# CoPE attention: the table selection as two row groups of 64 rows, with two table products and one addition moved on TensorE

## The chip, the cores and the metric

One Trainium2 chip, one of its cores. The metric is the device time of one execution of the whole program in microseconds (us), lower is better. Each kernel is run several times and the median counts.

## The reference

One decoder layer in float32: self-attention, cross-attention with contextual position encoding (CoPE), and a routed feed-forward layer. The change is in the cross-attention: batch 4, 1024 queries, 1024 keys, 16 heads of width 32, 64 positions.

```python
def cope(query, attn_logits, pos_emb):
    npos_max = pos_emb.shape[-1]
    gates = jax.nn.sigmoid(attn_logits)
    pos = jnp.flip(jnp.cumsum(jnp.flip(gates, axis=-1), axis=-1), axis=-1)
    pos = jnp.minimum(pos, npos_max - 1)
    pos_ceil = jnp.ceil(pos).astype(jnp.int32)
    pos_floor = jnp.floor(pos).astype(jnp.int32)
    logits_int = jnp.einsum('bhqd,dn->bhqn', query, pos_emb)
    logits_ceil = jnp.take_along_axis(logits_int, pos_ceil, axis=-1)
    logits_floor = jnp.take_along_axis(logits_int, pos_floor, axis=-1)
    w = pos - pos_floor
    return logits_ceil * w + logits_floor * (1.0 - w)
...
logits = jnp.einsum('bhqd,bhkd->bhqk', Q, K) / jnp.sqrt(jnp.asarray(d, Q.dtype))
scores = jax.nn.softmax(logits + cope(Q, logits, pos_emb), axis=-1)
out = jnp.einsum('bhqk,bhkd->bhqd', scores, V)
```

So every (query, key) pair looks up the curve `logits_int[query, :]` at its own position `pos`, between two neighbouring entries.

## The kernel before, in words

The program runs its stages one after the other; the CoPE attention (`build_cope_attention`) is the long one. It works through 128 **quads** (64 pairs of batch and head, two halves of 512 queries each), and a quad has four **slots** t = 0 to 3 of 128 queries. One number n = 4 i + t counts the slots. A PSUM or SBUF tile has 128 key rows as partitions and eight key groups along the free side.

Eight neighbouring keys share one *anchor*, a coarse position. For each query a small table is made by TensorE (`tables`: values, slopes and bends of its curve at 16 coarse places), kept by ScalarE (`keep_table`), and laid by DMA into `table[s]` with 128 rows: 8 lanes of 16 coarse places, each lane filled only for its own queries. VectorE makes one-hot rows `hot` out of the anchors (`compare`), and `pick` multiplies: 16 matmuls h = 0..15, with hot[:, h, :] as the 128-row stationary operand and 8 x 14 table columns as the moving one. The result in `pick_ps` holds 14 numbers for each pair of anchor and query. There is only one `pick_ps`: `pick` of slot n+1 waits until all products of slot n are made.

What each engine does in a slot t (in order, names as in the code):

- TensorE: `logits` of slot n-1, `values` of slot n-2, `add_cope` (adds the finished curve to the logits) of n-1, `turn_peak` and `bases` (turn row maxima for the softmax) of n-1, and `pick` of slot n+1. In t = 0, 1 four `gates` products of the next quad stand between them; in t = 2 `places` stands ahead of `pick`, and `turn_anchor` in its middle (`between`); in t = 3 two `tables` products.
- VectorE: `mux` (waits for `pick`), products 0 to 8 on `pick_ps`, among them `recip`, `top` (row maximum of the finished logits of n-1, then the addition of the curve's first value `start_at`), `top_row`, then `less`, and `compare` for a later `hot`, or in t = 2 `near` (rounds the positions of the next quad to anchors). In t = 3 one `compare` stands ahead of `less`, since the next `pick` needs its `hot`.
- GpSimd: `gather_up` (adds the eight parts of the curve), and per quad `link` twice and `spread` twice.
- ScalarE: gates, Relu terms (`past`), exponentials (`expo`), output scaling (`norm`), and the copies `keep_table` and `keep_anchor`.
- SyncE: all loads in one queue; `send_tables` and `load_table` bring the kept tables of quad i+2 into `table[s]`, `send_digits` and `load_hot` the anchors into `digits`.

`gate_ps` is one bank that `tables`, `gates`, `places` and `turn_anchor` use in turn.

## Time and profile before

| | |
|---|---|
| median of 3 runs | 13640.67 us (13613.76 to 13658.9) |
| the profiled execution | 13691.15 us, its span 13689.2 us |
| TensorE (PE) busy | 11636.6 us, 85% |
| VectorE (DVE) | 7724.8 us, 56% |
| GpSimd (POOL) | 6636.8 us, 48% |
| ScalarE (ACT) | 4384.1 us, 32% |
| mean granted TensorE clock | 0.889 |
| the costliest group | PE L929, the selection: 16384 matmul passes, 3311.4 us |

A float32 matmul appears as two records (passes) of PE, each with its own weight load (PEld), so the 16 matmuls of one `pick` are 32 rows. The busy time of PE is not its peak rate: ends of matmuls are modelled. A granted clock of 1.00 is 2.4 GHz, 0.50 is 1.2 GHz.

### The profile page before, as it was taken

The numbers are of one execution on the slowest core, as the hardware profiler recorded it, in microseconds if no ns is written. First come the engines' busy times: TensorE is split into PE (matmuls) and PEld (weight loads), VectorE is DVE, ScalarE is ACT, GpSimd is POOL, SyncE is SP. The second block draws the span as 40 slices with busy tenths as digits, with TensorE's granted clock in tenths as the row PEclk, the third lists the DMA queues.
The fourth block names the chain that finished last, engine by engine and source line by source line (L and its number), as shares of the span: only waits on it lengthen the run. The fifth ranks groups of instructions, "written<-read, shape, count | busy, mean of one in ns | idle before, by whom it ended". The sixth has DMA issues, their size and how long they took to land. (4 is left out here: it accounts for less than half of the span.)

```text
span 13689.2 us, 172386 instructions
## 1 busy us (share of the span) xinstructions
PE 11636.6 (85%) x54902; PEld 7795.5 (57%) x54902; DVE 7724.8 (56%) x14164; ACT 4384.1 (32%) x7378; POOL 6636.8 (48%) x5384
## 2 busy tenths in 40 slices
PE   8777899986688888888888888888888888888745
PEld 3555333334366666666666666666666666666521
DVE  0111444432266676667667766666667666666533
ACT  0011233321133333333333333333333333333210
POOL 0000000000077777777777777777777777777500
PEclk9789999987799999999999999999999999999866
DMA  3111222221111111111111111111111111111123
GB/s 76 47 46 43 74 76 76 76 65 61 58 38 40 42 42 38 39 42 41 40 38 41 42 42 37 40 42 41 40 38 42 41 41 37 40 42 41 36 70 104
DMA packets 1054791, 669.07 MB, mean 49 GB/s; under 512 B 804354, under 2 KB 846082, under 8 KB 1054738
## 3 DMA queue, kind: packets, MB, share of 16 engines
q1 hardware_dynamic: 981010, 659.99, 16.7%
q10 hardware_dynamic: 73728, 8.42, 0.4%
q8 instruction: 27, 0.44, 0.0%
q14 instruction: 26, 0.21, 0.0%
HBM read 482.28 MB, written 185.60 MB: 49 GB/s over the span
## 5 line engine op out<-in xcount | busy, mean ns | idle before, releaser
L1311 POOL TENSOR_TENSOR c_total<-c_total,c_over 128x384 f32<-128x384 f32 (+3 forms) x3584 | 3402.5, 949 | 400.0 <-DVE c_over L1211 123.0
L929 PE MATMUL c_pickps<-c_table,c_hot 128*128 128x112 f32 x16384 | 3311.4, 374 | 267.0 <-DVE c_hot L1180 258.8
L929 PEld LDWEIGHTS c_pickps<-c_table,c_hot 128*128 128x128 f32 x16384 | 3187.7, 223 | 529.8 <-issue 523.4
L1188 DVE COPY_PREDICATED c_pickps<-c_upper,c_pickps 128x256 f32<-128x256 uint32 (+1 forms) x1024 | 798.9, 826 | 2176.3 <-PE c_pickps L929 2176.3
L1278 POOL IOTA c_digitrow<- 1x128 f32 x1 | 0.3, 256 | 3678.7 <-POOLq L66 3678.7
L1311 POOL TENSOR_TENSOR c_total<-c_total,c_middle 128x1024 f32<-128x1024 f32 x512 | 1201.2, 2346 | 990.4 <-DVE c_middle L1202 990.2
L1062 ACT ACTIVATE c_over<-c_place,c_thresholds 128x384 f32<-128x384 f32 (+3 forms) x3584 | 1589.9, 526 | 0.0
L1211 DVE TENSOR_TENSOR c_over<-c_over,c_pickps 128x384 f32<-128x384 f32 (+3 forms) x3584 | 1437.2, 446 | 0.0
L1290 POOL TENSOR_TENSOR c_place<-c_place 128x512 f32<-128x512 f32 x768 | 977.2, 1272 | 774.5 <-ACT c_place L1050 733.0
L1299 POOL TENSOR_TENSOR c_place<-c_place 128x1024 f32<-128x1024 f32 (+1 forms) x512 | 1060.2, 2093 | 427.2 <-DVE c_place L1175 427.2
L947 PE MATMUL c_scoreps<-c_total,c_ident 128*128 128x512 f32 x2048 | 1237.1, 736 | 0.0
L902 PE MATMUL c_gateps<-c_qa,c_ka 128*128 128x512 f32 x2048 | 1107.8, 623 | 125.5 <-ACT c_place L1045 124.8
L1045 ACT ACTIVATE c_place<-c_gateps 128x512 f32<-128x512 f32 x1024 | 611.9, 598 | 1820.0 <-PE c_gateps L902 1819.8
L966 PEld LDWEIGHTS c_softps<-c_v,c_probs 128*128 128x128 f32 x8192 | 1012.8, 198 | 154.8 <-issue 120.8
L966 PE MATMUL c_softps<-c_v,c_probs 128*128 128x33 f32 x8192 | 1025.2, 281 | 2.7 <-ACT c_probs L1068 2.7
L1068 ACT ACTIVATE c_probs<-c_probs 128x1024 f32<-128x1024 f32 x512 | 540.3, 1055 | 1213.5 <-DVE c_probs L1227 1213.5
L567 ACT ACTIVATE a_probs<-a_turnedps 128x1024 f32<-128x1024 f32 x512 | 524.4, 1024 | 1073.3 <-PE a_turnedps L468 1073.3
L1215 DVE TENSOR_REDUCE c_peak<-c_scoreps 128x128 f32<-128x1024 f32 x512 | 626.0, 1223 | 357.3 <-PE c_scoreps L947 357.3
L954 PE MATMUL c_softps<-c_ident,c_peak 128*128 128x128 f32 x1024 | 260.7, 338 | 642.5 <-DVE c_peak L1217 642.5
L954 PEld LDWEIGHTS c_softps<-c_ident,c_peak 128*128 128x128 f32 x1024 | 159.8, 197 | 1104.3 <-DVE c_peak L1217 1104.3
L519 DVE TENSOR_REDUCE a_max<-a_peakps 128x1 f32<-128x1024 f32 x512 | 603.1, 1220 | 325.5 <-PE a_peakps L456 325.5
L1202 DVE SCALAR_TENSOR_TENSOR c_middle<-c_place,c_pickps 128x256 f32<-128x256 f32 x2048 | 719.6, 413 | 0.0
(210 smaller groups left out, 14100.7 us busy)
## 6 DMA issues: line engine op xcount, KB each, us to landing
c_digits<-t_digits SPq DMA_DIRECT2D x512, 256.0 KB
t_tables<-c_tablesb SPq DMA_DIRECT2D x256, 256.0 KB, 2.0
c_table<-t_tables SPq DMA_DIRECT2D x1024, 56.0 KB, 2.3
a_q<-t_qa SPq DMA_DIRECT2D x64, 512.0 KB
a_k<-t_ka SPq DMA_DIRECT2D x64, 512.0 KB
c_kb<-t_kb SPq DMA_DIRECT2D x256, 128.0 KB, 2.3
a_q<-t_qa SPq DMA_DIRECT2D x128, 128.0 KB, 2.4
a_k<-t_ka SPq DMA_DIRECT2D x128, 128.0 KB, 2.5
```

Of the source, the lines that this page charges most:

```text
L902: nc.tensor.matmul(gate_ps[:, :], k_a[:, key * 128:(key + 1) * 128], q_a[:, :], start=True, stop=True).then_inc(s_gateps, 1)
L929: mm = nc.tensor.matmul(pick_ps[:, h // 4, 0:WIDTH, r * 8:(r + 1) * 8], hot[t % 2][:, h, :], table[s][:, :, :, t * 16 + h].rearrange("p l ...
L947: mm = nc.tensor.matmul(score_ps[:, 4 * half:4 * half + 4, :], ident[:, :], total[x][:, 4 * half:4 * half + 4, :], start=False, stop=True)
L966: mm = nc.tensor.matmul(soft_ps[:, 256:256 + D_HEAD + 1], probs[x][:, key, :], v[s][:, key, :], start=(key == 0), stop=(key == 7))
L1062: ins = nc.scalar.activation(over[x][:, at:at + keys, :], place[s][:, key:key + keys, t * QT:(t + 1) * QT], ACT.Relu, scale=sign, bias=thr ...
L1188: ins = nc.vector.copy_predicated(pick_ps[:, :, at:at + width, :], far.unsqueeze(2).to_broadcast([128, 4, width, 32]), pick_ps[:, :, at + ...
L1202: ins = nc.vector.scalar_tensor_tensor(out=middle[x][:, :, b * 32:(b + 1) * 32], in0=here[:, :, b, :], scalar=-2.0, in1=pick_ps[:, b, 8, : ...
L1211: nc.vector.tensor_tensor(a, a, picked(col, keys), ALU.mult).then_inc(s_prod, 1)
L1215: nc.vector.tensor_reduce(peak[x][:, :], score_ps[:, :, :].rearrange("p k q -> p q k"), AX.X, ALU.max).then_inc(s_top, 1)
L1290: nc.gpsimd.tensor_tensor(place[s][:, slot, :], place[s][:, slot, :], place[s][:, prev, :], ALU.add).then_inc(s_chain, 1)
L1299: nc.gpsimd.tensor_tensor(a, place[s][:, 4:5, cols].to_broadcast([128, keys, 256]), a, op).then_inc(s_placed, 1)
L1311: nc.gpsimd.tensor_tensor(a, a, b, ALU.add).then_inc(s_add, 1)
```

## The change

Three edits:

1. `pick` issues, instead of 16 matmuls over 128 rows with 112 columns, 32 matmuls over 64 rows with 56 columns: for each h one in rows 0 to 63 (lanes 0 to 3) and one in rows 64 to 127 (lanes 4 to 7), which write different banks of `pick_ps`. For this the order of the 128 queries inside a slot changes, and with it the patterns of `keep_table` (four instructions instead of one) and of the anchors in `near` (two instead of one).
2. The two `tables` products of quad i+2 move from t = 3 (between `add_cope`, `turn_peak` and `bases`) to the place directly behind `logits`, one in t = 2 and one in t = 3. `places`, which uses the same bank, then waits for the first of the two copies.
3. `start_at` is no longer added to the row maxima by VectorE; TensorE multiplies both with the identity into the same accumulator.

```diff
-            def places(i, s):
+            def places(i, s, kept=None):
                 pe.wait_ge(s_gate, 8 * i + 8)
+                if kept is not None:
+                    pe.wait_ge(s_tablesb, kept)
                 pe.wait_ge(s_chain, LINKS * (i + 1))
...
                 for h in range(16):
                     if h == 8:
                         between()
-                    r = h % 4
-                    mm = nc.tensor.matmul(pick_ps[:, h // 4, 0:WIDTH, r * 8:(r + 1) * 8], hot[t % 2][:, h, :],
-                                          table[s][:, :, :, t * 16 + h].rearrange("p l m -> p m l"), start=True, stop=True)
+                    for g in range(2):
+                        rows, lanes = slice(64 * g, 64 * g + 64), slice(4 * g, 4 * g + 4)
+                        mm = nc.tensor.matmul(pick_ps[:, 2 * g + h // 8, 0:WIDTH, h % 8:32:8], hot[t % 2][rows, h, :],
+                                              table[s][rows, lanes, :, t * 16 + h].rearrange("p l m -> p m l"),
+                                              start=True, stop=True)
                 mm.then_inc(s_pickps, 1)
...
             def turn_peak(n, x):
+                after(pe, s_norm, n)
+                nc.tensor.matmul(soft_ps[:, 0:128], start_at[x][:, :], ident[:, :], start=True, stop=False)
                 pe.wait_ge(s_peak, n + 1)
-                after(pe, s_norm, n)
-                nc.tensor.matmul(soft_ps[:, 0:128], peak[x][:, :], ident[:, :], start=True, stop=True).then_inc(s_peakps, 1)
+                nc.tensor.matmul(soft_ps[:, 0:128], peak[x][:, :], ident[:, :], start=False, stop=True).then_inc(s_peakps, 1)
...
-                elif t == 3 and at in (1, 2) and not final(i, 2):
-                    tables(i + 2, at - 1)
+                elif t > 1 and at == 0 and not final(i, 2):
+                    tables(i + 2, t - 2)
...
-                nc.scalar.activation(table_sb[n][:, :].rearrange("p (l x) -> p l x", l=8), gate_ps[:, :].rearrange("p (x l) -> p l x", l=8),
-                                     ACT.Copy).then_inc(s_tablesb, 1)
+                kept = table_sb[n][:, :].rearrange("p (g l t e h) -> p g l t e h", g=2, l=4, t=4, e=2)
+                made = gate_ps[:, :].rearrange("p (t g e l h) -> p g l t e h", t=4, g=2, e=2, l=4)
+                for g in range(2):
+                    for e in range(2):
+                        ins = nc.scalar.activation(kept[:, g, :, :, e, :], made[:, g, :, :, e, :], ACT.Copy)
+                ins.then_inc(s_tablesb, 1)
...
-                nc.vector.tensor_scalar(anchor[:, :].rearrange("p (t l h) -> p t h l", t=4, l=8),
-                                        rounded[:, :].rearrange("p (t h l) -> p t h l", t=4, l=8), EIGHTS, None, ALU.subtract).then_inc(s_anchor, 1)
+                turned = anchor[:, :].rearrange("p (b l e h) -> p b l e h", l=4, e=2, h=8)
+                plain = rounded[:, :].rearrange("p (b e l h) -> p b l e h", l=4, e=2, h=8)
+                for e in range(2):
+                    ins = nc.vector.tensor_scalar(turned[:, :, :, e, :], plain[:, :, :, e, :], EIGHTS, None, ALU.subtract)
+                ins.then_inc(s_anchor, 1)
...
-                nc.vector.tensor_reduce(peak[x][:, :], score_ps[:, :, :].rearrange("p k q -> p q k"), AX.X, ALU.max).then_inc(s_top, 1)
-                dve.wait_ge(s_top, n + 1)
-                nc.vector.tensor_tensor(peak[x][:, :], peak[x][:, :], start_at[x][:, :], ALU.add).then_inc(s_peak, 1)
+                nc.vector.tensor_reduce(peak[x][:, :], score_ps[:, :, :].rearrange("p k q -> p q k"), AX.X, ALU.max).then_inc(s_peak, 1)
```

The order of TensorE in slot t = 3 of the first quad, from the second half of the selection of t = 3 to the selection of the next quad, before the change (x8: so many matmuls in a row):

```order
L929 MATMUL c_pickps<-c_table,c_hot 128x14x8 x8
L940 MATMUL c_scoreps<-c_qb,c_kb 128x128 x8
L966 MATMUL c_softps<-c_v,c_probs 128x33 x8
L947 MATMUL c_scoreps<-c_total,c_ident 128x512 x2
L893 MATMUL c_gateps<-c_qa,c_knots 128x512
L954 MATMUL c_softps<-c_ident,c_peak 128x128
L893 MATMUL c_gateps<-c_qa,c_knots 128x512
L958 MATMUL c_softps<-c_negident,c_rowmax 128x128
L929 MATMUL c_pickps<-c_table,c_hot 128x14x8 x16
```

The same stretch of TensorE after the change:

```order
L933 MATMUL c_pickps<-c_table,c_hot 128x56 x16
L945 MATMUL c_scoreps<-c_qb,c_kb 128x128 x8
L894 MATMUL c_gateps<-c_qa,c_knots 128x512
L972 MATMUL c_softps<-c_v,c_probs 128x33 x8
L952 MATMUL c_scoreps<-c_total,c_ident 128x512 x2
L958 MATMUL c_softps<-c_ident,c_start 128x128
L960 MATMUL c_softps<-c_ident,c_peak 128x128
L964 MATMUL c_softps<-c_negident,c_rowmax 128x128
L933 MATMUL c_pickps<-c_table,c_hot 128x56 x32
```

One table product stands behind the logits, the other has gone to slot t = 2, the start product stands ahead of the peak product, and the matmuls of a selection have doubled in number and halved in columns. Nothing is left between `add_cope` and the selection but `turn_peak` and `bases`.

## Rows read from the trace of the kernel before

**Rows 1.** The page: span, and granted clock in 40 slices (tenths).

```profile
span 13689.2 us, 172386 instructions
...
PEclk9789999987799999999999999999999999999866
```

**Rows 2.** By source line: VectorE's `mux`, two instructions a slot, first and last start.

```profile
L1188 DVE COPY_PREDICATED c_pickps<-c_upper,c_pickps x1024: 428/826/1230, 3763.1 to 12911.9; 128x256 f32<-128x256 uint32 x171
```

**Rows 3.** Timeline: `mux` of t=1, 2, 3, 0, 1 (start us, us, what; [idle before]).

```profile
8007.01 1.56 DVE L1188 COPY_PREDICATED c_pickps<-c_upper,c_pickps 128x256 f32<-128x256 uint32 x2 [4.69 <-PE c_pickps L929]
...
8023.60 1.56 DVE L1188 COPY_PREDICATED c_pickps<-c_upper,c_pickps 128x256 f32<-128x256 uint32 x2 [4.67 <-PE c_pickps L929]
...
8042.66 1.56 DVE L1188 COPY_PREDICATED c_pickps<-c_upper,c_pickps 128x256 f32<-128x256 uint32 x2 [3.26 <-PE c_pickps L929]
...
8061.58 1.56 DVE L1188 COPY_PREDICATED c_pickps<-c_upper,c_pickps 128x256 f32<-128x256 uint32 x2 [4.43 <-PE c_pickps L929]
...
8078.19 1.56 DVE L1188 COPY_PREDICATED c_pickps<-c_upper,c_pickps 128x256 f32<-128x256 uint32 x2 [4.69 <-PE c_pickps L929]
```

**Rows 4.** Timeline, TensorE at granted clock 1.00: loads of selection and logits, `add_cope`, values.

```profile
8000.53 5.98 PEld L929 LDWEIGHTS c_pickps<-c_table,c_hot 128*128 128x128 f32 x31 [0.24 <-issue]
...
8006.79 0.97 PEld L940 LDWEIGHTS c_scoreps<-c_qb,c_kb 32*128 32x128 f32 x16 [0.28 <-issue]
...
8010.54 1.96 PE L947 MATMUL c_scoreps<-c_total,c_ident 128*128 128x512 f32 x4
...
8024.47 1.86 PEld L966 LDWEIGHTS c_softps<-c_v,c_probs 128*128 128x128 f32 x16
```

**Rows 5.** Timeline, slot t=1: VectorE's `top` and last products; GpSimd's `gather_up`.

```profile
8012.54 1.22 DVE L1215 TENSOR_REDUCE c_peak<-c_scoreps 128x128 f32<-128x1024 f32 x1 [0.53 <-PE c_scoreps L947]
...
8013.80 0.29 DVE L1217 TENSOR_TENSOR c_peak<-c_peak,c_start 128x128 f32<-128x128 f32 x1
8013.94 7.21 POOL L1311 TENSOR_TENSOR c_total<-c_total,c_over 128x512 f32<-128x512 f32 x7
...
8015.01 1.27 DVE L1211 TENSOR_TENSOR c_over<-c_over,c_pickps 128x128 f32<-128x128 f32 x4
```

**Rows 6.** Timeline, slot t=2: wait for the peak, selection, `near`.

```profile
8030.64 0.49 PE L954 MATMUL c_softps<-c_ident,c_peak 128*128 128x128 f32 x2 [2.40 <-DVE c_peak L1217]
...
8035.17 3.29 PE L929 MATMUL c_pickps<-c_table,c_hot 128*128 128x112 f32 x16
...
8035.42 0.70 DVE L1162 TENSOR_SCALAR c_gateps<-c_gateps 128x512 f32<-128x512 f32 x1 [1.19 <-PE c_gateps L908]
...
8037.53 0.69 DVE L1170 SCALAR_TENSOR_TENSOR c_rounded<-c_rounded,c_gateps 128x512 f32<-128x512 f32 x1
```

**Rows 7.** Timeline, slot t=3: `add_cope`, `compare`, and the selection behind it.

```profile
8045.33 3.27 PE L947 MATMUL c_scoreps<-c_total,c_ident 128*128 128x512 f32 x4
...
8053.10 1.40 DVE L1180 TENSOR_SCALAR c_hot<-c_digits,c_digit 128x2048 f32<-128x2048 uint8 x1
...
8054.73 6.70 PE L929 MATMUL c_pickps<-c_table,c_hot 128*128 128x112 f32 x32 [2.11 <-DVE c_hot L1180]
```

**Rows 8.** Busy time by stretches: start:end, length, engines, granted clock (PEclk), DMA share, GB/s.

```profile
8042.50:8045.80 3.30, 3.30 (x34) 2.99 (x34) 3.10 (x5) 0.65 (x2) 1.21 (x1) 1.00 0.37 120
8045.90:8049.20 3.30, 3.30 (x5) 1.28 (x4) 2.32 (x7) 0.29 (x1) 2.04 (x1) 0.50 0.13 37
...
8056.20:8059.40 3.20, 3.20 (x17) 3.20 (x16) 0.95 (x1) 3.20 (x7) 3.12 (x3) 0.50 0.51 117
```

**Rows 9.** Timeline, the last slots, at low clock: logits, values, `add_cope`.

```profile
12922.11 1.79 PEld L940 LDWEIGHTS c_scoreps<-c_qb,c_kb 32*128 32x128 f32 x16 [2.35 <-DVE c_probs L1227]
...
12924.12 3.49 PEld L966 LDWEIGHTS c_softps<-c_v,c_probs 128*128 128x128 f32 x16 [0.22 <-issue]
...
12927.56 3.33 PE L947 MATMUL c_scoreps<-c_total,c_ident 128*128 128x512 f32 x4
```

**Rows 10.** Busy time by stretches, as above: the stretch of rows 9.

```profile
12922.00:12931.00 9.00, 8.77 (x36) 6.37 (x36) 0.30 (x3) 1.34 (x2) 2.47 (x4) 0.54 0.02 4
```

More of the change, by code:

```diff
@@ L758, in build_cope_attention @@
             sem(f"c_s{n}") for n in ("edge", "anchor", "near", "hot", "muxed", "start", "prod", "peak", "rowmax", "less", "rden"))
-        s_chain, s_placed, s_add, s_held, s_top = (sem(f"c_s{n}") for n in ("chain", "placed", "add", "held", "top"))
+        s_chain, s_placed, s_add, s_held = (sem(f"c_s{n}") for n in ("chain", "placed", "add", "held"))
         block = open_block(nc, ctx, sems)
@@ L889, in tables @@
                     pe.wait_ge(s_qka, 32 * (i + 1))
-                    after(pe, s_anchorsb, i)
+                    after(pe, s_gate, 8 * i)
                 else:
                     pe.wait_ge(s_tablesb, 2 * i + 1)
+                    after(pe, s_anchorsb, i)
                 nc.tensor.matmul(gate_ps[:, :], knots[:, 8 * n:8 * n + 8, :].rearrange("p m a -> p (m a)"), q_a[:, :],
@@ L1004, in step @@
                     if t == 2 and ahead:
-                        places(i + 1, 1 - s)
+                        places(i + 1, 1 - s, None if final(i, 2) else 2 * i + 5)
                     def between():
@@ L1021, in _ @@
             turn_anchor(0)
+            pe.wait_ge(s_anchorsb, 1)
             for n in range(2):
@@ L1087, in aside @@
                             gate(i + 1, 1 - s, 4 * t + at)
-                        elif t == 3 and at in (1, 2) and not final(i, 2):
-                            keep_table(i + 2, at - 1)
+                        elif t > 1 and at == 0 and not final(i, 2):
+                            keep_table(i + 2, t - 2)
                     aside(0)
```

## The prediction

> **What bounds the kernel now.** I read the page first. The CoPE attention is the long stage: `mux` starts 1024 times, twice a slot, from 3763.1 to 12911.9 us [rows 2]. That is 9148.8 us for 511 slots, so 17.90 us a slot and 71.6 us a quad, two thirds of the span of 13689.2 us [rows 1]. The rest of the program is not touched.
>
> Then I read one quad in the timeline [rows 3]. From `mux` to `mux` it takes 16.59 us (t=1), 19.06 (t=2), 18.92 (t=3) and 16.61 (t=0). In each slot VectorE sits idle for 3.3 to 4.7 us until the selection ends, and the next selection may start only when VectorE has made the last product. So TensorE's selection and a phase of VectorE and TensorE together take turns on the single `pick_ps`. Shortening either shortens the slot.
>
> The phase between selections has its own chain. In t=1 `add_cope` releases `top` 5.53 us after `mux` (12.54 against 7.01), `top` takes 1.22, the addition ends 7.08 after `mux`, the last products 9.27 after it [rows 5]. TensorE has to turn the peak and do two more gate products after that, so its own work ends the phase, about 10.1 us after `mux` (16.6 minus a selection of 6.48, next paragraph). In t=3 the end is `compare`: 53.10 + 1.40, then the selection at 54.73 [rows 7].
>
> **The selection.** It starts at 8000.53 and `mux` at 8007.01: 6.48 us [rows 3, 4]. Its weight loads follow each other at (5.98 - 0.20) / 30 = 0.193 us. The values, also 128 rows but 33 columns, go at (1.86 - 0.19) / 15 = 0.111, and the logits, which already alternate between two row groups, do a pair of loads in (0.97 - 0.19) / 7 = 0.111 [rows 4]. So a load costs 0.111, the rest of 0.193 is the 112 columns, and two row groups run side by side. With 56 columns half of 0.193 (0.097) is below the load, so I take 0.111 for a pair: 31 x 0.111 plus 0.45 to `mux` = 3.9 us. Gain 2.57 us a slot. The bounds are 0.097 a pair (0.4 us less a slot, which would need faster loads than any row has, so I exclude it) and 0.111 a single matmul, if 64-row groups did not overlap (64 x 0.111 + 0.45 = 7.6, which is 1.1 more than now).
>
> The Trainium skill (TensorE: Matmul & The Clock Gate, part 3, what overlaps) says that a weight load overlaps a running matmul only when the row groups differ. By that rule load and columns of one group would add up, 0.111 plus about 0.04 to 0.08, and a new selection would take some 5 us and not 3.9. The trace disagrees: values with 128 rows keep 0.111 although each load follows a matmul in the same rows [rows 4].
>
> **The moved parts.** The addition of the curve's first value leaves VectorE: 0.29 us in t=1 [rows 5], on the chain, so 0.3 a slot. Its replacement on TensorE, two passes of 0.111, stands ahead of the wait for the peak, which is 2.40 us in t=2 [rows 6]; hidden there, and costing 0.2 if that wait were gone. The table products go ahead of `values`, so `add_cope` comes in t=2 and t=3 where it comes in t=1 behind a gate product: `top` 5.53 us after `mux`. `keep_table` grows from one instruction to four on ScalarE, at most 1 us more, twice a quad. ScalarE has slack, and the waiting `places` comes 6 us later; it costs that 1 us if the slack is gone. The anchors as two instructions add about 0.25 us to `near`. GpSimd's sums end at 8021.15 in t=1 (13.94 + 7.21 [rows 5]); they start with VectorE's products and `link`, which do not get shorter, so they end 3.0 us after the next `mux`, when `add_cope` comes at 3.5. It just fits.
>
> **The clock decides the rest.** The granted clock is not 1.00 all through [rows 1]. It was 0.50 from 8045.9 to 8049.2, after 3.3 us in which TensorE was busy all the time, but with logits (32 rows) and values (33 columns), and again from 8056.2 to 8059.4, after the wait for `compare` [rows 7, 8]. At low clock `add_cope` takes 3.27 or 3.33 us in place of 1.96, the loads of the logits 1.79 for 0.97 (a pair at 0.213), the values 3.49 for 1.86 [rows 4, 7, 9]. The old selection hardly feels it: 6.70 us with half of it at low clock against the 5.98 of loads and tail of 0.35 at full [rows 4, 7, 8]. The new one does, since 0.213 is far above 0.111: 31 x 0.213 + 0.5 = 7.1 us. Whether the clock would rise again during a new selection no row shows. The bounds are the old selection, in which it rose, and logits plus values, through which it stayed low (mean 0.54 [rows 10]). The new one has half the rows and half the columns in each matmul, so I take it nearer to the second: the low clock lasts through a new selection and what follows, until `add_cope`.
>
> **A quad, slot by slot**, from `mux` to `mux`:
>
> - t=1, full clock: 16.6 - 2.57 - 0.3 = 13.7.
> - t=2: `top` ends at 6.75, two products and `top_row` put `bases` at 7.9 and `places` at 8.1, four passes of 0.43 end at 9.8, half a selection from 9.9 to 11.7. `near` starts at 10.4, when `less` is done, and its fourth step ends 2.8 (35.42 to 38.22 [rows 6]) plus 0.25 later: 13.5. TensorE now waits 1.8 us there, where before the half selection (3.29 us [rows 6]) covered it. Then 0.9 for `turn_anchor`, 1.8 for the other half, 0.4: 16.7. If the clock falls in that hole, 0.8 and 1.6 more: 19.1.
> - t=3: products end at 9.0, `compare` at 10.4, the selection starts at 10.6. TensorE has almost nothing to do for 5 us ahead of it, more than before, so the selection runs at low clock: 10.6 + 7.1 = 17.7. If the clock was low since t=2, logits, table, values and `add_cope` add 0.8 + 0.8 + 1.6 + 1.4, and some 0.3 on the small ones: 22.6.
> - t=0, low clock from the selection on: 13.7 + 0.8 + 0.8 + 1.6 + 1.4 + 0.7 for the second gate product = 19.0.
>
> The short quad is 13.7 + 16.7 + 17.7 + 19.0 = 67.1, the long one 13.7 + 19.1 + 22.6 + 19.0 = 74.4. Which comes depends on whether the clock falls in the hole at the anchors. Nothing in the trace says how often. I take them as equally frequent: 70.7, which is 0.9 less than 71.6, times 128 quads = 115 us less than the profiled 13691 us, so 13576. The median of the runs is 50 us below the profiled execution, so I forecast 13525 us.
>
> **Rivals.**
> - *Short quads only*: 67.1 to 68.3 a quad, 430 to 570 us less: 13070 to 13210 us. For it: the hole of 1.8 us is shorter than the one ahead of `compare`. Against: half a selection on each side of it is thin work too. 0.22.
> - *The clock keeps up, or rises during the new selection.* All at full clock: 13.7 + 13.7 + 16.7 + (10.6 + 3.9) = 58.6, 13.0 less a quad, 11980 us; with a rise halfway some 12500. The rows of the fall ahead of 8045.9 speak against it. 0.10. The Trainium skill (same page, part 1) ties the fall to an idle engine; by that rule a slot with such short waits as here would stay warm and this rival would be the forecast. The trace disagrees: busy 3.30 of 3.30 us, then 0.50 [rows 8].
> - *The clock falls at the anchors in every quad*, and the kernel is slower: 74.4, 2.8 more a quad, 350 us, 13990 us. It decides from six long quads in ten on, where (71.6 - 67.1) / 7.3 is passed. 0.26.
> - *Row groups of 64 do not overlap*, or the clock falls inside each selection and stays low in t=1 and t=0 too: 1.1 more in each slot, less the 0.3, is 3.2 a quad or 14050 us; with the second some 6 us a slot, up to 16000. Against: the logits overlap. 0.07.
> - The forecast itself, both kinds mixed, 13300 to 13750: 0.35.
>
> **Numbers.** A measurement of this kernel tells 0.3% (41 us) from no change. The range from 12950 to 14200 holds the short, mixed and long cases, 0.83; it leaves out the full clock and the slowest. The forecast's own range is 13300 to 13750. Faster: 0.10 + 0.22 + 0.20 of the mixed case = 0.52; within 0.3%: 0.08; slower: 0.26 + 0.07 + 0.07 of the mixed case = 0.40.
>
> **What would show it.** Right: selections of 3.9 us in t=1 and t=2 by pairs at 0.11; a selection near 7 us ahead of t=0; PEclk below 0.91 in the stage; TensorE waiting for `near` inside the selection of t=2; no VectorE addition. Wrong: loads of a pair at 0.19 or more at full clock; a selection of t=3 below 5 us; a clock that is low in t=1; or the slot ended by GpSimd's sums, which have 0.5 us to spare.

## The result and the profile after

| | before | after |
|---|---|---|
| median | 13641.18 us, 4 runs (13613.76 to 13658.9) | 14054.81 us, 4 runs (13932.39 to 14078.61) |
| profiled execution | 13691.15 us | 14078.61 us, its span 14076.8 us |
| mean granted TensorE clock | 0.889 | 0.788 |

The ratio of after to before is 1.0287, with a 95% interval of 1.0224 to 1.035. The kernel is slower by 414 us. The range held it (12950 to 14200), but the forecast of 13525 us stood on the wrong side of no change.

From the page of after: span; busy time; granted clock in 40 slices; the queue that fetches instructions (packets, MB, share); and the costliest TensorE group, the selection (busy us, mean ns of one).

```profile
span 14076.8 us, 207201 instructions
...
PE 12004.7 (85%) x72310; PEld 7964.7 (57%) x72310; DVE 7634.5 (54%) x13780; ACT 4401.1 (31%) x8146; POOL 6629.7 (47%) x5384
...
PEclk9788999977777777777787787777777777777666
...
q8 instruction: 643, 10.53, 0.3%
...
L933 PE MATMUL c_pickps<-c_table,c_hot 64*128 64x56 f32 x32768 | 2580.4, 330 | 283.6 <-DVE c_hot L1194 177.4
```

Two things stand out beside [rows 1]. The stage that ran at nine tenths of the clock now runs between seven and eight tenths, and the instruction queue moved 10.53 MB. On the page of before that queue's line reads

```profile
q8 instruction: 27, 0.44, 0.0%
```

The selection itself did get cheaper: 2580.4 us busy, from 3311.4.

By source line, `mux` of after (two instructions a slot, duration min/median/max, first and last start):

```profile
L1202 DVE COPY_PREDICATED c_pickps<-c_upper,c_pickps x1024: 428/826/1228, 3756.8 to 13293.2; 128x256 f32<-128x256 uint32 x171
```

(13293.2 - 3756.8) / 511 x 4 = 74.65 us a quad, 3.03 more than the 71.62 of [rows 2]; times 128 that is 388 us, nearly the whole loss. Timeline of after, `mux` of t=0, 1, 2, 3, 0, which answers to [rows 3]:

```profile
8004.43 1.56 DVE L1202 COPY_PREDICATED c_pickps<-c_upper,c_pickps 128x256 f32<-128x256 uint32 x2 [4.81 <-PE c_pickps L933]
...
8025.36 1.56 DVE L1202 COPY_PREDICATED c_pickps<-c_upper,c_pickps 128x256 f32<-128x256 uint32 x2 [2.00 <-PE c_pickps L933]
...
8039.24 1.56 DVE L1202 COPY_PREDICATED c_pickps<-c_upper,c_pickps 128x256 f32<-128x256 uint32 x2 [2.29 <-PE c_pickps L933]
...
8060.07 1.56 DVE L1202 COPY_PREDICATED c_pickps<-c_upper,c_pickps 128x256 f32<-128x256 uint32 x2 [4.49 <-PE c_pickps L933]
...
8082.98 0.43 DVE L1202 COPY_PREDICATED c_pickps<-c_upper,c_pickps 128x256 f32<-128x256 uint32 x1 [4.81 <-PE c_pickps L933]
```

The slots take 20.93 us (t=0), 13.88 (t=1), 20.83 (t=2) and 22.91 (t=3). Only t=1 became shorter as planned. The timeline of TensorE over the same slots shows why (start, us, what; [idle before]); it answers to [rows 4], [rows 6] and [rows 7]:

```profile
8006.24 2.08 PE L945 MATMUL c_scoreps<-c_qb,c_kb 32*128 32x128 f32 x16 [1.97 <-issue]
...
8021.40 3.81 PE L933 MATMUL c_pickps<-c_table,c_hot 64*128 64x56 f32 x64
...
8046.04 0.49 PE L960 MATMUL c_softps<-c_ident,c_peak 128*128 128x128 f32 x2 [1.09 <-DVE c_peak L1229]
8047.04 0.49 PE L964 MATMUL c_softps<-c_negident,c_rowmax 128*128 128x128 f32 x2 [0.51 <-DVE c_rowmax L1233]
8047.36 1.99 PE L910 MATMUL c_gateps<-c_place,c_before 128*128 128x512 f32 x2
8049.14 1.86 PE L911 MATMUL c_gateps<-c_place,c_upto 128*128 128x512 f32 x2
8050.93 2.02 PE L933 MATMUL c_pickps<-c_table,c_hot 64*128 64x56 f32 x32
8054.23 2.08 PE L917 MATMUL c_gateps<-c_ident,c_anchor 128*128 128x128 f32 x8 [1.28 <-DVE c_rounded L1184]
8056.24 3.67 PE L933 MATMUL c_pickps<-c_table,c_hot 64*128 64x56 f32 x32
8059.84 2.08 PE L945 MATMUL c_scoreps<-c_qb,c_kb 32*128 32x128 f32 x16
...
8066.98 3.76 PE L952 MATMUL c_scoreps<-c_total,c_ident 128*128 128x512 f32 x4
...
8072.06 0.49 PE L960 MATMUL c_softps<-c_ident,c_peak 128*128 128x128 f32 x2 [0.89 <-DVE c_peak L1229]
...
8075.74 7.08 PE L933 MATMUL c_pickps<-c_table,c_hot 64*128 64x56 f32 x64 [2.20 <-DVE c_hot L1194]
```

A selection is 64 passes in 3.81 us in t=1. In t=2 `places` goes at half speed (1.99 and 1.86 us), the first half of the selection at full speed again (2.02 us). After the wait for `near` (1.28 us, L1184) `turn_anchor` takes 2.08 and the second half 3.67, then everything up to `add_cope` (3.76 for four passes, against 1.96) runs at half speed. The selection at the end of t=3 takes 7.08 us. By stretches (start:end, length, busy time of each engine, granted clock, DMA share, GB/s), as in [rows 8]:

```profile
8039.00:8046.50 7.50, 6.41 (x44) 4.49 (x42) 6.71 (x13) 3.75 (x9) 6.72 (x8) 1.00 0.01 2
8047.40:8050.90 3.50, 3.50 (x6) 1.05 (x4) 2.19 (x5) 1.06 (x1) 3.27 (x4) 0.51 0.02 5
...
8059.80:8070.90 11.10, 11.10 (x42) 7.72 (x40) 5.18 (x11) 1.30 (x6) 3.70 (x3) 0.50 0.42 128
...
8075.80:8082.00 6.20, 6.20 (x60) 6.20 (x60) 2.36 (x2) 4.07 (x8) 5.96 (x6) 0.50 0.12 45
```

The clock is at 1.2 GHz for 11.10 us in which TensorE was busy for 11.10 us, so a busy engine does not bring it back up here. I counted 122 quads of the stage from the starts of `mux` and the granted clock behind them. In 82 of them t=3 begins at low clock, and such a quad takes 77.6 us; the other 40 take 68.7. Before, t=3 began at full clock in all 122, although the clock had been low for two thirds of `places` or more in every one (mean 0.50 to 0.67). In both kernels the clock mostly comes back behind `places`: over the first half of the selection it has a mean of 0.95 before, and of 0.89 in the 82 quads of after. What differs comes next. Before, `turn_anchor` and the second half ran at full clock in all 122; in the 82 of after `turn_anchor` ran at low clock in 68, and the second half in all.

The first row of TensorE's timeline is a second find: TensorE waits 1.97 us inside t=0 for its own instructions ("issue"). All such waits of TensorE ahead of the logits, from the list of waits of after (us in total, times, longest):

```profile
PE c_scoreps L945 <- issue: 115.7, 61, 2.5
```

61 times is once for every jump back of the loop, which makes 62 turns of two quads. Before, no matmul of this line waited for issue; only its loads did, 0.3 us each (143.0 us in 511 times).

### The profile page after: what moved, and what is told of

It reads as the page before. It is cut to its first block and busy times, and to the rows that moved or that the text cites. A ratio compares the mean times of both kernels' runs of the same rounds, so it can differ in the third digit from the quotient of the medians.

```text
span 14076.8 us, 207201 instructions
## 1 busy us (share of the span) xinstructions
PE 12004.7 (85%) x72310; PEld 7964.7 (57%) x72310; DVE 7634.5 (54%) x13780; ACT 4401.1 (31%) x8146; POOL 6629.7 (47%) x5384
## 3 DMA queue, kind: packets, MB, share of 16 engines
q8 instruction: 643, 10.53, 0.3%
## 5 line engine op out<-in xcount | busy, mean ns | idle before, releaser
L933 PEld LDWEIGHTS c_pickps<-c_table,c_hot 64*128 64x128 f32 x32768 | 2476.3, 238 | 685.9 <-issue 673.4
L933 PE MATMUL c_pickps<-c_table,c_hot 64*128 64x56 f32 x32768 | 2580.4, 330 | 283.6 <-DVE c_hot L1194 177.4
L972 PEld LDWEIGHTS c_softps<-c_v,c_probs 128*128 128x128 f32 x8192 | 1366.7, 252 | 362.2 <-issue 359.0
L903 PE MATMUL c_gateps<-c_qa,c_ka 128*128 128x512 f32 x2048 | 1293.1, 718 | 140.4 <-ACT c_place L1056 138.5
L952 PE MATMUL c_scoreps<-c_total,c_ident 128*128 128x512 f32 x2048 | 1383.5, 812 | 0.0
L972 PE MATMUL c_softps<-c_v,c_probs 128*128 128x33 f32 x8192 | 1304.1, 323 | 2.7 <-ACT c_probs L1079 2.7
L945 PE MATMUL c_scoreps<-c_qb,c_kb 32*128 32x128 f32 x8192 | 792.6, 348 | 117.5 <-issue 115.7
L945 PEld LDWEIGHTS c_scoreps<-c_qb,c_kb 32*128 32x128 f32 x8192 | 672.8, 244 | 170.3 <-issue 126.0
L1194 DVE TENSOR_SCALAR c_hot<-c_digits,c_digit 128x2048 f32<-128x2048 uint8 x512 | 723.8, 1414 | 10.1 <-DMA c_digits<-t_digits 10.1
```

The source lines that it names most:

```text
L903: nc.tensor.matmul(gate_ps[:, :], k_a[:, key * 128:(key + 1) * 128], q_a[:, :], start=True, stop=True).then_inc(s_gateps, 1)
L933: mm = nc.tensor.matmul(pick_ps[:, 2 * g + h // 8, 0:WIDTH, h % 8:32:8], hot[t % 2][rows, h, :], table[s][rows, lanes, :, t * 16 + h].rear ...
L945: mm = nc.tensor.matmul(score_ps[:, key, :], k_b[s][at:at + D_HEAD, key * 128:(key + 1) * 128], q_b[s][at:at + D_HEAD, t * QT:(t + 1) * QT ...
L952: mm = nc.tensor.matmul(score_ps[:, 4 * half:4 * half + 4, :], ident[:, :], total[x][:, 4 * half:4 * half + 4, :], start=False, stop=True)
L972: mm = nc.tensor.matmul(soft_ps[:, 256:256 + D_HEAD + 1], probs[x][:, key, :], v[s][:, key, :], start=(key == 0), stop=(key == 7))
L1194: nc.vector.tensor_scalar(hot[x][:, :, :], digits[x][:, :, :], digit[:, :], None, ALU.is_equal).then_inc(s_hot, 1)
```

## The experiments

I held three theories. **Clock:** the fall at the wait for the anchors lasts through t=3 and t=0, and makes the loss. **Row groups:** half matmuls are themselves no gain on the whole path, whatever the clock. **Fetch:** the instructions of TensorE's loop body are brought in anew in every turn. In the expectations below the first is theory C, the third theory F, and theory A its later form, in which the place of the body counts too; rival M is that the moved table products do the harm, and theory S that a VectorE addition waits for GpSimd. Twelve kernels tell them apart. The fillers in some of them are matmuls whose result nobody reads; the rest of each computation is unchanged.

In the slot times below t=0 is the one behind the selection that ends t=3, each a mean over some 120 quads of the profiled run. Before has 16.61, 16.59, 19.73 and 18.72 us in t=0 to t=3, after has 20.34, 13.87, 19.24 and 21.27. So the change wins 2.7 us in t=1 and 0.5 in t=2, and loses 3.7 in t=0 and 2.6 in t=3.

### One edit at a time

`groups_only` is edit 1 alone (edits 2 and 3 undone), `moves_only` edits 2 and 3 with the old selection:

```diff
-                elif t > 1 and at == 0 and not final(i, 2):
-                    tables(i + 2, t - 2)
+                elif t == 3 and at in (1, 2) and not final(i, 2):
+                    tables(i + 2, at - 1)
...
+                dve.wait_ge(s_top, n + 1)
+                nc.vector.tensor_tensor(peak[x][:, :], peak[x][:, :], start_at[x][:, :], ALU.add).then_inc(s_peak, 1)
```

> Only the first edit: the selection in two row groups with its new query order; table products and the addition of the first value as before. Theory C (the selection in row groups is short at full clock, 3.9 us, but 7 us at low clock, and the low clock then lasts until add_cope of the next slot): the harm is in this edit alone, so this kernel is slower than before too, about 14100 to 14400 us; without a table product behind the logits the clock falls at least as often as in the changed kernel. Rival M (the moved table products and the split copies do the harm, the row groups gain): below 13600 us. Theory F (the longer loop body makes TensorE fetch its instructions again once every two quads): its instruction queue still moves some 10 MB, as in the changed kernel.

Measured: 14182.8 us, ratio 1.0395 [1.0369, 1.0421]; 75.9 us a quad (t=0 20.28, t=1 17.12, t=2 20.96, t=3 17.52). That t=1 is 3.3 us longer than in after is taken up under `compact`. The loss lies elsewhere than in after: t=3 is short and begins at low clock in only 14 of 122 quads, but the clock is low in much of t=2 (mean 0.67, against 0.85 in after) and at the start of t=0 in 115 of 122. The instruction queue moved 9.54 MB.

> Only the second and third edit, the selection as before with 128 rows. Theory C: no harm; the addition off VectorE's chain gives 0.3 to 0.7 us a slot, so 13400 to 13600 us. Rival M (the moved products do the harm): above 13750 us. Theory F: the instruction queue moves about as little as before (0.44 MB), and no wait for issue ahead of the logits.

Measured: 13203.65 us, ratio 0.969 [0.9661, 0.9718]; 68.3 us a quad (16.29, 16.27, 17.92, 17.78). So the whole loss belongs to edit 1: it costs 4.2 us a quad alone (71.7 to 75.9) and 6.4 on top of the other two (68.3 to 74.7). Edits 2 and 3 gain 3.4 us a quad beside the old selection, more than was expected, but only 1.2 beside the new one (75.9 to 74.7).

`peak_only` is the kernel before with edit 3 alone:

```diff
             def turn_peak(n, x):
+                after(pe, s_norm, n)
+                nc.tensor.matmul(soft_ps[:, 0:128], start_at[x][:, :], ident[:, :], start=True, stop=False)
                 pe.wait_ge(s_peak, n + 1)
-                after(pe, s_norm, n)
-                nc.tensor.matmul(soft_ps[:, 0:128], peak[x][:, :], ident[:, :], start=True, stop=True).then_inc(s_peakps, 1)
+                nc.tensor.matmul(soft_ps[:, 0:128], peak[x][:, :], ident[:, :], start=False, stop=True).then_inc(s_peakps, 1)
...
-                dve.wait_ge(s_top, n + 1)
-                nc.vector.tensor_tensor(peak[x][:, :], peak[x][:, :], start_at[x][:, :], ALU.add).then_inc(s_peak, 1)
```

> The kernel before with the third edit alone: the curve's first value added by TensorE. Forecast's price: 0.3 us a slot, 1.2 us a quad, 150 us in all, so 13480 us. Theory S (the addition, with two operands in SBUF, also waits for a running addition of GpSimd, as in compact, where it took 2.37 us beside a GpSimd operation of 2.34 us): its worth is its mean duration of 0.52 us in the kernel before plus what it held up, some 2 us a quad, 13350 to 13430 us. If the moved table products are what gave moves_only its 3.1%, this kernel stays above 13550 us.

Measured: 13268.02 us, ratio 0.9712 [0.967, 0.9753]; 68.6 us a quad. Edit 3 is worth 3.1 us a quad and edit 2 the last 0.3. Of the 3.1, t=0 and t=1 give 0.32 each, t=2 1.5 and t=3 0.9. The reason is in the timeline of before, the addition in t=2 and t=3, where it took nearly three and nearly four times the 0.29 us of t=1 [rows 5]:

```profile
8029.77 0.82 DVE L1217 TENSOR_TENSOR c_peak<-c_peak,c_start 128x128 f32<-128x128 f32 x1
...
8049.89 1.10 DVE L1217 TENSOR_TENSOR c_peak<-c_peak,c_start 128x128 f32<-128x128 f32 x1
```

TensorE's waits for the peak in the list of waits, of before:

```profile
PE c_softps L954 <- DVE c_peak L1217: 642.5, 501, 2.6
```

and of `peak_only`:

```profile
PE c_softps L955 <- DVE c_peak L1216: 197.8, 440, 1.3
```

That is 445 us less waiting, of which 395 us came out of the span (13689.2 to 13294.0).

### Filling the wait at the anchors

`fill_anchor` is after plus four matmuls of 256 columns ahead of `turn_anchor`, into a bank of `pick_ps` that the second half of the selection overwrites. They take 1.99 us (below), somewhat longer than the wait that they fill (1.28 in the row above), so by themselves they can only cost time.

```diff
+            def fill(out, count):
+                for _ in range(count):
+                    nc.tensor.matmul(out, ident[:, :], knots[:, :, :].rearrange("p m a -> p (m a)"), start=True, stop=True)
...
                         if t == 2 and ahead:
+                            fill(pick_ps[:, 1, 0:8, :].rearrange("p m r -> p (m r)"), 4)
                             turn_anchor(i + 1)
```

> The changed kernel plus four matmuls of 256 columns without a use (about 1.7 us at full clock) ahead of turn_anchor inside the selection of t=2, where TensorE waits for near. They write a bank of pick_ps that the second half of the selection overwrites. Theory C: the clock no longer falls there, only ahead of t=0, so every quad becomes the short kind: 16.7 (t=2), 17.9 (t=3), about 20 (t=0), 13.9 (t=1) = 68.5 in place of 74.7 us, about 13250 us. Rival (the time is in the work and the patterns, the clock only follows): 14050 us or some 0.1 to 0.5% more for the added work.

Measured: 13421.31 us, ratio 0.9838 [0.9814, 0.9863]; 69.7 us a quad (20.11, 13.87, 17.91, 17.78). Timeline of TensorE, the same place as above:

```profile
8044.80 1.09 PE L910 MATMUL c_gateps<-c_place,c_before 128*128 128x512 f32 x2
8045.72 1.02 PE L911 MATMUL c_gateps<-c_place,c_upto 128*128 128x512 f32 x2
8046.67 2.02 PE L933 MATMUL c_pickps<-c_table,c_hot 64*128 64x56 f32 x32
8048.63 1.99 PE L958 MATMUL c_pickps<-c_knots,c_ident 128*128 128x256 f32 x8
8050.46 1.05 PE L917 MATMUL c_gateps<-c_ident,c_anchor 128*128 128x128 f32 x8
8051.44 2.02 PE L933 MATMUL c_pickps<-c_table,c_hot 64*128 64x56 f32 x32
...
8057.15 1.96 PE L952 MATMUL c_scoreps<-c_total,c_ident 128*128 128x512 f32 x4
...
8064.19 7.08 PE L933 MATMUL c_pickps<-c_table,c_hot 64*128 64x56 f32 x64 [2.28 <-DMA c_table<-t_tables]
```

2 us a quad of matmuls that nobody needs make the kernel 4.4% faster (0.9838 / 1.0287), and turn it from 2.9% slower to 1.6% faster than before. The clock is at full speed at the start of t=3 in all 122 quads (40 of 122 in after), and t=3 falls from 21.27 to 17.78 us. This is the clock theory shown at the place that it named: in 54 of the 122 `places` still ran at low clock, and t=3 began at full clock behind it all the same, so it is the wait for the anchors that decides. The expected 13250 us were missed, since t=2 took 17.91 us and not 16.7: the fillers cost 1.2 us over a short t=2 of after (16.76). And the selection ahead of t=0 still takes 7.08 us, and t=0 20.11.

`fill_all` adds fillers where TensorE waits for the peak, the row maximum and `compare` in t=2 and t=3:

```diff
+                    if t == 2 and not final(i, 2):
+                        pe.wait_ge(s_tablesb, 2 * i + 5)
+                        fill(gate_ps[:, 0:256], 3)
+                    if t == 3 and not final(i, 2):
+                        pe.wait_ge(s_tablesb, 2 * i + 6)
+                        fill(gate_ps[:, 0:256], 3)
...
+                    if t == 2 and not final(i, 2):
+                        fill(gate_ps[:, 0:256], 1)
+                    if t == 3 and not final(i, 2):
+                        fill(gate_ps[:, 0:256], 1)
...
+                    if t == 3 and not final(i, 2):
+                        fill(gate_ps[:, 0:256], 5)
```

> The same four matmuls, and more without a use in the waits of TensorE in t=2 and t=3: three ahead of the peak, one ahead of bases, and five ahead of the selection of t=3, all into the free gate_ps. Theory C: the clock stays at 1.00 through nearly the whole stage, the selection ahead of t=0 takes 3.9 us, a quad 13.9 + 16.7 + 14.5 + 14.9 = 60 us, about 12180 us (12050 to 12500). Rival (work and patterns): 14100 to 14400 us, since there is more work. Theory F: once every two quads some 2 us of waiting for issue stay, ahead of the logits of t=0.

Measured: 12774.07 us, ratio 0.9367 [0.9328, 0.9407]; 64.7 us a quad. t=1 to t=3 take 13.87, 16.96 and 14.60 us, at full clock throughout. But t=0 takes 13.87 us in one quad of each turn and 24.8 in the other. Two rows of TensorE's timeline in such a slot say what stands there:

```profile
7942.32 0.97 PE L945 MATMUL c_scoreps<-c_qb,c_kb 32*128 32x128 f32 x10 [2.89 <-issue]
7945.30 1.22 PE L945 MATMUL c_scoreps<-c_qb,c_kb 32*128 32x128 f32 x6 [2.01 <-issue]
```

4.9 us of waiting for instructions, and behind it the low clock (the gate product that follows takes 2.08 us). So the expected 12180 us were missed, and the fetch that theory F named is what stands in the way.

`moves_fill` puts the same fillers (two in place of three ahead of the peak, none at the anchors) on the old selection, to see what they give without edit 1:

```diff
+                    if t == 3 and not final(i, 2):
+                        pe.wait_ge(s_tablesb, 2 * i + 6)
+                        fill(gate_ps[:, 0:256], 2)
```

> moves_only (no row groups) with matmuls without a use in t=2 (2 and 1) and t=3 (2, 1 and 5). Theory C: the clock stays up, but the old selection hardly feels it and add_cope is at full clock already there, so little is won: t=3 17.1 in place of 17.8 us, t=2 17.6, a quad 67.3 us, 13080 us (within 1% of moves_only). If filling alone gave the 9% of fill_all, this would be near 12500 us.

Measured: 13079.05 us, ratio 0.9601 [0.9566, 0.9635], only 0.9% below `moves_only`, although the clock rose from 0.915 to 0.948. The old selection hardly feels the clock, as the prediction argued; the new one does.

### Row groups where the clock is up

`hybrid` keeps the row groups for the selections of t=1 and t=2, which start at full clock, and does those of t=0 and t=3 over 128 rows (the copies of tables and anchors are split to match):

```diff
+                    if t in (0, 3):
+                        r = h % 4
+                        mm = nc.tensor.matmul(pick_ps[:, h // 4, 0:WIDTH, r * 8:(r + 1) * 8], hot[t % 2][:, h, :],
+                                              table[s][:, :, :, t * 16 + h].rearrange("p l m -> p m l"), start=True, stop=True)
+                        continue
                     for g in range(2):
```

> The changed kernel with row groups only for the selections of t=1 and t=2, which run at full clock in every kernel so far; those of t=0 and t=3 as before, over 128 rows, with the old query order in their 128 columns. About 1640 records of TensorE in the loop body against 1353 (before) and 1865 or more (the kernels that fetched instructions). Theory C: slots 13.9, 13.9, 17.9 and 17.8 us as in moves_only for the last two, a quad 63.5 us, about 12600 us. Theory F: the instruction queue falls back to 0.44 MB if the body now fits, or stays at some 9 MB with about 4 us of waiting for issue every two quads if it does not (then 12900 us or more).

Measured: 13179.21 us, ratio 0.9671 [0.9638, 0.9705]; 68.2 us a quad. t=1 takes 13.87 us, against 16.27 in `moves_only`: at full clock the row groups gain 2.4 us a slot, and the theory that they are no gain falls. t=0 again takes 13.87 us in one quad and 20.7 in the other, and the page has the queue q8 at 9.49 MB. By the trace a turn of TensorE's loop has 1637 instructions here (four to a matmul, and 69 that wait, count and branch), 256 fewer than after's 1893, and was still fetched.

`hybrid_fill` is `hybrid` with the fillers of `fill_all` but those at the anchors, 1745 instructions:

```diff
+                        fill(gate_ps[:, 0:256], 3)
```

> The same with the matmuls without a use in the waits of t=2 and t=3 (3 and 1; 3, 1 and 5), about 1720 records in the body. Theory C: the clock stays up also ahead of t=0; the selections there last 6.3 us, so only 0.7 us a quad less than hybrid, about 12500 us. Theory F as for hybrid.

Measured: 12609.33 us, ratio 0.9241 [0.9201, 0.9281]; 63.2 us a quad (13.87, 13.87, 18.27, 17.19). From its page:

```profile
PEclk9788899997779999999999999999999999999766
...
q8 instruction: 31, 0.51, 0.0%
```

The longer body was not fetched, the shorter one was. So length alone does not decide.

`wide3_fill` is `hybrid_fill` with row groups for t=0, 1 and 2:

```diff
-                    if t in (0, 3):
+                    if t in (3,):
```

> Row groups for t=0, 1, 2, only the selection of t=3 (with turn_anchor in its middle) over 128 rows, so that its first half covers near; matmuls without a use in t=2 and t=3 as in fill_all, none at the anchors. About 1845 records in the body. Theory C: 13.9, 13.9, 17.2 and 14.6 us, a quad 59.6 us if no instructions are fetched: 12100 us. Theory F: if the body is too long, every second t=0 slot is some 25 us as in fill_all, 65 us a quad, 12800 us; rival to F (the wait ahead of the logits comes with the row groups of 64 rows standing before row groups of 32): the same 65 us, and hybrid, whose t=0 selection has 128 rows, has none whatever its length.

Measured: 12792.67 us, ratio 0.9389 [0.9356, 0.9422]; 64.8 us a quad, t=3 down to 14.59, but with 1873 instructions fetched again (q8 at 9.54 MB), t=0 13.87 and 22.6 in turn.

### Where the loop lies

The packets of q8 are 16 KB (10.53 MB / 643). I took each as a block of 256 instructions; the last section says how well that fits. Counted between the jumps back in the trace, a turn of the loop fetches ten of them on average in after, nine in every turn of `hybrid`. I took it that the body stays when it touches seven such blocks or fewer, and is fetched anew, all of it, when it touches eight or more. A body of 1637 or 1745 instructions then touches seven or eight, as it lies. To try this, the loop was moved and nothing else: 76 instructions (19 matmuls of one column) ahead of `hybrid`'s loop, 100 ahead of `hybrid_fill`'s.

```diff
+            for _ in range(19):
+                nc.tensor.matmul(gate_ps[:, 0:1], ident[:, :], ones[:, 0:1], start=True, stop=True)
             for n in range(2):
```

> Exactly the loop of hybrid, with 19 matmuls of one column ahead of the loop, once in the program (some 5 us), which move TensorE's loop body by 76 instructions in its code. hybrid fetched 9.49 MB of instructions although hybrid_fill, with a longer body, fetched 0.51 MB, so the length alone (theory F as first put) does not decide it. Theory A (the fetch happens when the body, from where it happens to start, touches one more block of 16 KB than is kept: 7 by my count of the code): the body now touches 7 instead of 8, the instruction queue moves about 0.5 MB, t=0 is 13.9 us always, a quad 64.9 in place of 68.2 us, about 12750 us. Rival (something in hybrid's order of work makes the wait for issue): no change from 13179 us beyond 0.3%.

Measured: 12785.51 us, ratio 0.9382 [0.9345, 0.942], which is 3.0% below `hybrid` though it executes more; 64.8 us a quad, with t=0 at 13.87 in every quad. The fetch is gone. Pages, `hybrid` first:

```profile
q8 instruction: 579, 9.49, 0.3%
```

then `hybrid_shift`:

```profile
q8 instruction: 31, 0.51, 0.0%
```

And the logits of t=0, one turn of each in the timeline, `hybrid`:

```profile
7975.58 0.94 PE L950 MATMUL c_scoreps<-c_qb,c_kb 32*128 32x128 f32 x12
7978.66 0.80 PE L950 MATMUL c_scoreps<-c_qb,c_kb 32*128 32x128 f32 x4 [2.15 <-issue]
7979.39 2.08 PE L903 MATMUL c_gateps<-c_qa,c_ka 128*128 128x512 f32 x2
```

and `hybrid_shift`:

```profile
7981.80 1.16 PE L950 MATMUL c_scoreps<-c_qb,c_kb 32*128 32x128 f32 x16
7982.89 1.13 PE L903 MATMUL c_gateps<-c_qa,c_ka 128*128 128x512 f32 x2
```

A wait of 2.15 us in the first, and the gate product behind it at low clock (2.08 for 1.13). On average over the turns, 2.1 us of waiting became 6.9 in that slot.

> The reverse: the loop of hybrid_fill, which fetched nothing, moved by 25 matmuls of one column (100 instructions) ahead of the loop. Theory A: it now touches 8 blocks, the instruction queue moves some 9.5 MB, every second t=0 slot waits some 4 us for issue and then runs at low clock, 63.2 grows to about 66.5 us a quad, about 13030 us. Rival: 12609 us as before.

Measured: 12688.67 us, ratio 0.9303 [0.927, 0.9336]; q8 581 packets and 9.52 MB. The same move brought the fetch into a kernel that had none, as expected, but it cost 0.8 us a quad and not the 3.3 that I gave it: TensorE waited at most 1.0 us there and the clock mostly stayed up (mean 0.95 in the t=0 of those quads, 0.77 in `hybrid`). Whether a body is fetched is explained; how long TensorE waits for it (0.3 to 4.3 us a turn on average over these kernels) is not.

`compact` was to have everything: row groups for t=0, 1, 2, no fetch (1767 instructions, placed by 41 such matmuls), bigger and fewer fillers in t=3, and, to save instructions, edit 3 undone:

```diff
             def turn_peak(n, x):
+                pe.wait_ge(s_peak, n + 1)
                 after(pe, s_norm, n)
-                nc.tensor.matmul(soft_ps[:, 0:128], start_at[x][:, :], ident[:, :], start=True, stop=False)
-                pe.wait_ge(s_peak, n + 1)
-                nc.tensor.matmul(soft_ps[:, 0:128], peak[x][:, :], ident[:, :], start=False, stop=True).then_inc(s_peakps, 1)
+                nc.tensor.matmul(soft_ps[:, 0:128], peak[x][:, :], ident[:, :], start=True, stop=True).then_inc(s_peakps, 1)
...
+                nc.vector.tensor_tensor(peak[x][:, :], peak[x][:, :], start_at[x][:, :], ALU.add).then_inc(s_peak, 1)
```

> The change made to fit: row groups for the selections of t=0, 1, 2, the one of t=3 over 128 rows (its first half covers near); table products behind the logits; the first value added by VectorE again (32 instructions less in the body); three matmuls without a use of 512 columns in t=3 (one ahead of the peak, two ahead of the selection); 41 matmuls of one column ahead of the loop so that the body lies within 7 blocks. Theory A with theory C: no fetch, t=0 and t=1 14.2 us, t=2 18.2, t=3 15.3, a quad 61.9 us, about 12350 us, the fastest so far. If three are too few to keep the clock up, the selection ahead of t=0 takes 7 us and t=0 19 us: 70 us a quad, 13400 us. If the body still touches 8 blocks: 65 us, 12800 us.

Measured: 13255.81 us, ratio 0.9725 [0.9684, 0.9765]; 68.3 us a quad. There was no fetch (q8 0.52 MB), but the expected time was missed by 7%. t=1 took 17.50 us in place of 13.87 and t=2 21.91. The timeline of t=1 has it:

```profile
8020.68 2.34 POOL L1346 TENSOR_TENSOR c_total<-c_total,c_middle 128x1024 f32<-128x1024 f32 x1
...
8020.80 2.37 DVE L1252 TENSOR_TENSOR c_peak<-c_peak,c_start 128x128 f32<-128x128 f32 x1
...
8023.22 0.54 PE L968 MATMUL c_softps<-c_ident,c_peak 128*128 128x128 f32 x2 [2.86 <-DVE c_peak L1252]
8023.55 1.92 PE L903 MATMUL c_gateps<-c_qa,c_ka 128*128 128x512 f32 x2
```

An addition of 0.29 us took 2.37, until 0.15 us after the end of GpSimd's instruction, which had begun 0.12 us ahead of it. With the faster slots the two meet in every t=1 and t=2 (mean 2.33 and 2.37 us). In `groups_only`, which has the addition too, it takes 2.32 us on average in t=1. That is 2.3 of the 3.6 us by which t=1 is longer; behind the wait for it the clock falls, and the gate product takes 1.92 us for 1.03. t=2 has no fillers here, so its 21.91 us are not the addition's alone. Edit 3 is what keeps this wait out of the short slots, and I had taken out the wrong thing.

The Trainium skill says why (SBUF — State Buffer, SBUF: two separate sides): a VectorE instruction with two SBUF inputs and a GpSimd instruction that reads SBUF exclude each other for a whole instruction. The trace agrees for VectorE's side, with 2.37 us beside 2.34; GpSimd's side is not shown here.

## Why the prediction was wrong

**What held.** The new selection goes by pairs at 0.11 and `mux` follows 3.96 us after its start (3.9 forecast). At low clock `mux` follows after 7.24 us (7.1; the passes take 7.08). t=1 is 13.87 us (13.7) at full clock. The clock is low through the last selection and in t=0 until `add_cope` (0.50 from 8004.43 to 8016.00 us). TensorE waits for `near` inside the selection of t=2, 1.28 us. Quads are of two kinds, and which one comes is decided by whether t=3 begins at low clock.

**The steps that failed** are two. The first is "Nothing in the trace says how often. I take them as equally frequent". 82 of 122 quads are long, 67%, which passes the limit of six in ten that the prediction itself gave, and so the sign turned. `fill_anchor` shows that this place decides, since without the wait there none of 122 is long. But with 67% and the sizes as forecast a quad would be 0.33 x 67.1 + 0.67 x 74.4 = 72.0 us, 0.4 more than before or some 50 us in all. The larger part of the 414 us is the second step, the sizes of the slots t=0 and t=2 in that sum. Two of the rivals gave a time near 14055 us: "the clock falls at the anchors in every quad" (13990) had the mechanism, for two quads in three; "row groups of 64 do not overlap" (14050) came nearest only by chance, for its mechanism fell.

**Mis-sized terms.** Short quads took 68.7 us, not 67.1; long ones 77.6, not 74.4. From 70.7 to the measured 74.7 a quad, the share of long ones makes 0.17 x 7.3 = 1.2 us and the sizes 0.33 x 1.6 + 0.67 x 3.2 = 2.7. Of these 2.7, t=0 makes 1.3, t=2 0.9, t=3 0.3 and t=1 0.2:
- t=0: 20.2 us in short quads and 20.4 in long ones, for 19.0. By turns of the loop it is 19.6 in one quad and 21.0 in the other. The 1.4 us between them is the fetch of TensorE's loop, a term that the sum did not have. By these means it is 0.7 us a quad, some 90 of the 414 us. I did not run after with its body shortened to seven blocks, so this share is read from the trace and not tested by itself.
- t=2 of a long quad: 20.4 us for 19.1. In 76 of the 82 the clock is low already in `places` (1.99 and 1.86 us, for the 1.09 and 1.02 that `fill_anchor` shows at full clock), 5.6 us before the wait that I had named (8047.36 against the end of the half selection at 8052.95). It mostly comes back for the half selection, and falls again behind the wait. The forecast had only this second stretch. In short quads t=2 is 16.76 us, as forecast (16.7).
- t=3 of a long quad: 22.9 for 22.6; of a short one 17.9 for 17.7.

**Edit 3** was priced at 0.3 us a slot from the one row of t=1. In t=0 and t=1 that is what it is worth (0.32 in `peak_only`), but in t=2 and t=3 it is 1.5 and 0.9, as the rows of 0.82 and 1.10 us in the same timeline could have told. The sum did not suffer by it, since its t=2 and t=3 were built on the chain of t=1 and so never held the long additions.

**GpSimd's sums** were to end 3.0 us behind the next `mux`. That does not follow from the row given for it, which ends 14.14 us after its own `mux` and so 0.4 after a slot of 13.7. Nothing hung on it: in after the sums of t=1 end 2.35 us behind the `mux` at 8039.24, and `add_cope` comes at 3.52.

**Row groups that do not overlap** fell: 64 passes in 3.81 us. **The clock keeps up** fell too, by the window at 0.50 with 11.10 of 11.10 us busy. Its time of 11980 us was not reached; the nearest is `hybrid_fill` with 12609.33 us, which is 7.6% faster than before and 10% faster than after, and the best version found. It has edits 2 and 3, row groups in half of the selections, and thirteen matmuls a quad without a use that keep the clock up.

## What to carry to other kernels

Splitting a matmul into pieces that load TensorE less may shorten the instruction stream and still lose, if the work before and behind it lives at the edge of the clock's fall: read the granted clock by stretches, count how many rounds are at each level, and try a few useless matmuls in the wait that precedes the fall, since they are the cheapest test and sometimes the fix. When a change adds instructions to a loop, look at the instruction queue's line on the page: there a few thousandths of the DMA time stood for a wait in every turn, and moving the loop by 76 instructions removed it. Price a small VectorE instruction from every place where it runs beside GpSimd, not from one.

## What the runs showed of the hardware

- **TensorE's loop is fetched anew in each turn when it is long or lies badly.** All fourteen kernels fit one rule: a body that touches up to seven blocks of 16 KB stays; one that touches eight is fetched with nine packets a turn, one that touches nine, as after's does, with ten. The trace does not give the address at which the program begins, so this is a fit: with the loop of before beginning between 0.32 and 0.40 of the way into a block, the count comes out right for all fourteen. Of block sizes from 128 to 396 instructions in steps of four, the only other that fits is 228 with up to eight blocks staying, and for a far narrower choice of starts (6 of 228, against 22 of 256). The two shifts were forecast by the rule before they ran. The Trainium skill (Runtime: NRT & Kernel Launch, Instruction fetch mechanics) gives TensorE room for 2048 instructions in blocks of 256, which is eight blocks. The traces have the bodies that touch eight blocks fetched, `hybrid`'s 1637 instructions among them, so the room that counts for a loop here is a block less, in whole blocks. The same section says that "A taken branch whose target isn't in the current 2-page window forces a DMA fetch of the target page". The traces disagree for TensorE: a body of six blocks, before's 1353 instructions, is not fetched again in any turn (27 packets in the whole program).
- **A wait for instructions costs more than its length.** On average 2.1 us of it in `hybrid` made 6.9 us of slot and 4.3 in `fill_all` made 10.9, with the clock low behind it (gate product 2.08 us for 1.13); in `hybrid_fill_shift`, with at most 1.0 us, 1.4.
- **A VectorE addition with both operands in SBUF waits for a running GpSimd addition:** 0.29 us became 2.37 in `compact`, where it ended 0.15 us behind GpSimd's (the median of the 122 quads, in t=1 as in t=2).
- **The low clock costs the new selection more than the old one.** In row groups it takes 7.08 us at 0.50 for 3.81 at full clock. The old one with half of it at low clock took 6.85 us from its start to `mux` [rows 3, 7], 0.4 more than the 6.48 at full clock [rows 3, 4].
